# Two 16-head self attentions rebuilt: values as matmul weights in column groups, scores ahead of transposes, softmax by biased exponentials with their own row sums

## The reference, cut to what matters

```python
scores = jnp.einsum('bthd,bshd->bhts', q, k)
scores = scores * jnp.tril(jnp.ones((T, T)))
attn = jax.nn.softmax(scores / T ** 0.5, axis=-1)
out = jnp.einsum('bhts,bshd->bthd', attn, v).reshape(B, T, H * Dh)
return out @ Wo
```

```python
scores = jnp.einsum('bhqd,bhkd->bhqk', q, k) * 32 ** -0.5
attn = jax.nn.softmax(scores, axis=-1)
out = jnp.einsum('bhqk,bhkd->bhqd', attn, v)
return lora_linear(out.transpose(0, 2, 1, 3).reshape(B, L, H * hd), Wo, bo, Bo, Ao)
```

## Time and profile before

| | us |
|---|---|
| median of 3 runs (2780.65 to 2783.71) | 2782.24 |
| profiled execution, device time | 2780.92 |
| its span | 2779.2 |
| first attention: scores from, last exponentials to | 202.8, 308.3 |
| second attention: scores from, last exponentials to | 1587.8, 1698.3 |

### The profile page before, as it was taken

One profiled execution on the slowest core, in us unless ns is written; L12 is line 12 of the kernel. 1 busy time (PEld: TensorE's weight loads), 2 busy tenths in 40 slices (PEclk: granted clock), 3 DMA queues, 4 the chain that ended last, 5 costly groups with the idle time before them and its releaser, 6 DMA issues. The chain is left out here.

```text
span 2779.2 us, 48345 instructions
## 1 busy us (share of the span) xinstructions
PE 2516.6 (91%) x14891; PEld 2020.3 (73%) x14892; DVE 1668.5 (60%) x3141; ACT 1132.1 (41%) x2442; POOL 932.6 (34%) x942
## 2 busy tenths in 40 slices
PE   7999778769899989799997998998999999899998
PEld 7888655558688877578875777774665678788887
DVE  4537746669776656667675566864434325666564
ACT  2113256623343324455453133755555521444443
POOL 4213101124332235422333111753333322355555
PEclk9999889889899979899998898999999989999999
DMA  5444132125522045477774432344222031566664
GB/s 190 154 143 101 27 101 67 45 83 163 175 75 64 14 144 186 131 220 228 198 219 108 112 78 77 115 134 145 74 63 76 20 130 55 153 163 163 162 152 83
DMA packets 289277, 332.88 MB, mean 120 GB/s; under 512 B 147445, under 2 KB 202693, under 8 KB 287312
## 3 DMA queue, kind: packets, MB, share of 16 engines
q1 hardware_dynamic: 217904, 252.57, 28.9%
q0 software_dynamic: 20640, 51.74, 9.3%
q10 hardware_dynamic: 50560, 26.34, 3.3%
HBM read 233.86 MB, written 96.72 MB: 119 GB/s over the span
## 5 line engine op out<-in xcount | busy, mean ns | idle before, releaser
L898 PE MATMUL e_psum<-e_up_hi,hT_hi 128*128 x672 | 245.5, 365 | 21.3 <-DVE hT_lo L867 16.3
L900 PE MATMUL e_psum<-e_up_hi,hT_lo 128*128 x672 | 237.1, 353 | 0.0
L899 PE MATMUL e_psum<-e_up_lo,hT_hi 128*128 x672 | 236.5, 352 | 0.0
L1905 POOL TENSOR_TENSOR joint_a_p<-joint_a_p,joint_a_rinv 112x487 f32<-112x487 f32 x128 | 125.2, 999 | 196.1 <-DVE joint_a_rinv L1951 195.7
L1565 POOL TENSOR_TENSOR self_a_p<-self_a_p,self_a_mx 112x448 f32<-112x448 f32 x96 | 96.0, 1000 | 207.7 <-DVE self_a_mx L1622 207.7
L898 PEld LDWEIGHTS e_psum<-e_up_hi,hT_hi 128*128 128x128 f32 x672 | 127.7, 190 | 44.0 <-issue 32.6
L1956 DVE TENSOR_REDUCE joint_a_mx<-joint_psum 112x1 f32<-112x487 f32 x128 | 85.0, 664 | 122.1 <-PE joint_psum L1926 122.0
L794 ACT ACTIVATE e_gate<-e_psum 128x352 f32<-128x352 f32 (+1 forms) x86 | 44.4, 516 | 256.5 <-PE e_psum L900 256.0
L873 DVE TENSOR_TENSOR hT_lo<-e_psum,hT_hi 128x256 fp32r<-128x256 f32 (+2 forms) x138 | 55.6, 434 | 142.1 <-ACT hT_hi L812 142.1
L1656 ACT ACTIVATE self_a_p<-self_a_p 112x448 f32<-112x448 f32 x128 | 71.6, 575 | 165.7 <-POOL self_a_p L1565 115.4
L900 PEld LDWEIGHTS e_psum<-e_up_hi,hT_lo 128*128 128x128 f32 x672 | 127.6, 190 | 11.5
(11 more groups left out here) (565 smaller groups left out, 7419.9 us busy)
## 6 DMA issues: line engine op xcount, KB each, us to landing
e_up_raw<-in_L_ffn_w SPq DMA_DIRECT2D x64, 512.0 KB, 5.0
e_up_raw<-in_L_ffn_w SPq DMA_DIRECT2D x64, 352.0 KB, 3.7
e_dn_raw<-in_L_ffn_w SPq DMA_DIRECT2D x16, 1024.0 KB, 5.5
q_all<-p_p_t_stage ACTq DMA_DIRECT2D x56, 256.0 KB, 2.3
e_dn_raw<-in_L_ffn_w SPq DMA_DIRECT2D x16, 512.0 KB, 4.0
x_q<-q_all SPq DMA_DIRECT2D x8, 896.0 KB, 5.1
v_ctx<-front_c_v_stage SPq DMA_DIRECT2D x24, 250.0 KB
x_others<-k_ctx SPq DMA_DIRECT2D x8, 750.0 KB, 4.9
```

The costliest lines, as they stand in the source:

```text
L898: pe.matmul(out, lhs[0], rhs[0], start=k == 0, stop=False)
L899: pe.matmul(out, lhs[0], rhs[1], start=False, stop=False)
L900: return pe.matmul(out, lhs[1], rhs[0], start=False, stop=k == n_k - 1)
L1905: pool.tensor_tensor(p[:, r, :], p[:, r, :], rinv[:, r:r + 1].to_broadcast([T, S]), ALU.mult).then_inc(p_ready, 1)
```

## The change

Both attentions use a new class, `HeadSelfAttentionPart`; `QkvPart`, `OutNormPart` and the order function are the same. It differs so:

- **Order.** In A of step s PE has the scores of s first and the transposes of s-2 behind.
- **Softmax.** DVE takes the maxima and multiplies them by -scale (`neg`, 112x4). ACT takes one exponential per head, 112x112, with `neg` as bias and the row sum as its accumulator: eight per step instead of two. With a mask it reads the masked copy in SBUF, without one it reads the scores' banks in PSUM, so there the next scores wait for `exp_done` (before: for DVE's subtraction).
- **Row sums.** In B of the next step DVE inverts eight sums at once, and POOL multiplies both items by them, in both attentions. The transposes wait for POOL (`p_ready`).
- **Values.** V becomes the weights (112x32 per head), the transposed probabilities stream, and the heads of four items go to four 32-row groups of one PSUM bank. It is done once per sequence, in B of odd steps, and gives the result already transposed: `OutNormPart` then skips L2268 (`turned`), and the ones' column goes.

```diff
+class HeadSelfAttentionPart:
+        def gpsimd(pool):
...
+                yield
+                for i in pair(step, 1):
+                    pool.wait_ge(rinv_ready, i // W + 1)
+                    pool.tensor_tensor(p[:, i % RING, :, :], p[:, i % RING, :, :], rinv[:, i % RING, :].unsqueeze(2).to_broadcast([T, group, T]),
+                                       ALU.mult).then_inc(p_ready, 1)
...
+        def tensor(pe):
...
+                both = pair(step)
+                if both:
...
+                    reuse(pe, mask_done if mask else exp_done, both[-1] - N_S + 1)
+                    for j in range(group):
+                        for i in both:
+                            last = pe.matmul(ps[0:T, s_banks[i % N_S], j * T:(j + 1) * T], q[rows_of(i), b % 2, j, :],
+                                             k[rows_of(i), b % 2, j, :], start=True, stop=True)
...
+                for i in pair(step, LT):
+                    pe.wait_ge(p_ready, i + 1)
+                    reuse(pe, pt_ready, i - N_T + 1)
+                    for j in range(group):
+                        last = pe.transpose(ps[0:T, t_banks[i % N_T], j * T:(j + 1) * T], p[:, i % RING, j, :], core.ident[0:T, 0:T])
...
+                yield
+                at = step - LT
+                if at >= 0 and at % n_steps == n_steps - 1:
...
+                    pe.wait_ge(pt_ready, (b + 1) * n_items)
+                    for j in range(group):
+                        for i in range(b * n_items, (b + 1) * n_items):
+                            h = j * group + i % n_items
+                            last = pe.matmul(ps[rows_of(i), o_banks[b % N_O], j * T:(j + 1) * T], v[:, b % 2, h * dh:(h + 1) * dh],
+                                             pt[:, i % PT, j, :], start=True, stop=True)
+                    last.then_inc(pv_done, 1)
...
+        def vector(dve):
...
+                    dve.tensor_reduce(mx[:, i % RING, :], src, AX.X, ALU.max).then_inc(mx_ready, 1)
+                    dve.wait_ge(mx_ready, i + 1)
+                    dve.tensor_scalar(neg[:, i % RING, :], mx[:, i % RING, :], -scale, None, ALU.mult).then_inc(neg_ready, 1)
+                yield
+                before = pair(step, 1)
+                if before:
+                    at = before[0] % RING
+                    dve.wait_ge(exp_done, before[-1] + 1)
+                    dve.reciprocal(rinv[:, at:at + W, :], rsum[:, at:at + W, :]).then_inc(rinv_ready, 1)
...
+        def scalar(act):
...
+                yield
+                for i in pair(step):
+                    act.wait_ge(neg_ready, i + 1)
...
+                    for j in range(group):
+                        src = p[:, i % RING, j, :] if mask else ps[0:T, s_banks[i % N_S], j * T:(j + 1) * T]
+                        last = act.activation(p[:, i % RING, j, :], src, ACT.Exp, bias=neg[:, i % RING, j:j + 1], scale=scale,
+                                              accum_out=rsum[:, i % RING, j:j + 1])
+                    last.then_inc(exp_done, 1)
...
-                    a = SelfAttentionPart(g, "a", *head_qkv(p), float(T) ** -0.5, (2, 3), (4, 5), (6, 7), "tril", ALU.mult)
+                    a = HeadSelfAttentionPart(g, "a", *head_qkv(p), float(T) ** -0.5, (2, 3), (4, 5), (6, 7), "tril")
...
-                a = SelfAttentionPart(g, "a", *head_qkv(p), 32.0 ** -0.5, (2, 3), (4, 5), (6, 7))
+                a = HeadSelfAttentionPart(g, "a", *head_qkv(p), 32.0 ** -0.5, (2, 3), (4, 5), (6, 7))
```

101 lines of the change are left out of this document (100 added, 1 removed).

## The result

The changed kernel takes 2823.42 us (median of 3 runs, 2822.01 to 2829.43) against 2782.24 before: a ratio of 1.0159 (95% interval 1.0134 to 1.0183), 41 us slower. The forecast was 2797, with a range of 2777 to 2817. The direction was right; the size was not, and it lies outside the range.

What follows compares the result with a forecast made beforehand. PE was taken to bound the second attention's steps 6 to 15, DVE the first's. Span 2779.2 + 5.5 (second) + 3.7 (first) + 7 (clock) = 2795.4, given as 2797 us in measured time; range 2777 to 2817.

Steps and rivals of the forecast that it cites:

- The clock: Both attentions' loops: 38 us of PE work at full clock, about a fifth as much again at 1.2 GHz: +7, range 0 to 30.
- vanish, since PE waits: Second attention, steps 6 to 15: PE's saving of 3.4 us per sequence brings nothing, because PE waits.
- Behind step 15: Stretch from step 15's scores to the last transposes: +0.8 us in the first attention, +1.0 in the second.
- POOL's leg: POOL multiplies two items by the inverted sums before the transposes: 1.83 us; the first attention's last step pays it again, +0.8.
- Second attention, steps 6 to 15: Loop from scores through exponentials to next scores: 5.2 us even, 5.7 odd, 8.6 turn steps; 62.3 us against 53.6, +8.7.
- The wait for the banks: Second attention: next scores need both PSUM banks, which ACT's exponentials of the step before still read; closes the 5.2 us loop.
- First attention, steps 6 to 15: Cycle of two steps 14.2 instead of 12.73 us, DVE waiting 2.1 us at each turn step: +5.1.
- Exponentials: ACT, one per head at 112 columns with accumulator: 0.33 us each, eight in 2.66 a step; range 0.2 to 0.56.
- start: Before step 6, PE's shorter values save time: -2.2 us in the first attention, -4.2 in the second.
- The scores' place: Scores ahead of the transposes on PE: said to cost PE nothing.
- The sums: Span 2779.2 + 5.5 + 3.7 + 7 = 2795.4; with 1.7 above span and 1.3 to the median, given as 2797 us.
- The rival that named the half clock for most of the stretch: PE stays at 1.2 GHz (+19), or exponentials cost 0.45 us and more (+9, second attention): 2810 to 2820, chance 0.16.

Runs made afterwards that it cites:

- h6_filled_less: Changed kernel plus idle PE transposes where PE waits, also behind step 15, with 8 instead of 22 before the second attention's odd-step scores: 2796.83 us (1.0050).
- e5_early_sums: Changed kernel, but DVE inverts the previous step's sums at the end of its piece A instead of in piece B: 2809.98 us (1.0095).
- h3_filled_tail: Changed kernel plus idle PE transposes in steps 6 to 15 (22 before the second attention's odd-step scores) and behind step 15: 2801.46 us (1.0066).
- h2_filled: Changed kernel with early sums, DVE's subtraction, values and V's load a step later, plus 8 idle transposes before every step's scores from 6: 2794.38 us (1.0039).
- e4_subtracted: Changed kernel, but in the second attention DVE subtracts the maxima into SBUF, so the next scores wait for DVE, not the exponentials: 2807.78 us (1.0089).
- h5_second_unfilled: First attention as before the change; second rebuilt with early sums and DVE's subtraction, no idle transposes: 2780.78 us (0.9993 of the kernel before).

## Why the prediction was wrong

- **The clock: the step that failed.** "I take about a fifth, +7; the range is 0 to 30." Measured: 23, that is 0.6 of the 38 us of PE's work that I had counted in the loops. My own rows gave the pieces: waits of some 3 us, and the earlier trace rows, where one wait of 1.69 us was followed by 4.44 us of matmuls at mostly half clock. With waits of 1.5 to 3.8 us ahead of seven of the nine scores of steps 7 to 15, the second attention ran at 1.2 GHz for 0.6 of the stretch, not for a fifth. And the overall range, up to 2817, did not reach the end of the clock's own range, because I gave that end little chance.
- **PE as bound again.** The forecast took PE out of the reckoning ("vanish, since PE waits"). Mostly at half clock PE needs 7.4 and 7.6 us in the even steps without a turn and sets their length; at full clock (h6_filled_less) such a step took 5.4, for a loop of 5.2.
- **Behind step 15**: forecast +0.8 and +1.0, measured +9.1 and +8.5; with PE's waits filled still +7.2 and +4.1. This is the second term that was mis-sized. I counted POOL's leg, and gave the wait ahead of it nothing: the reciprocal of step 15's sums stands behind `hT_lo` of step 16 on DVE (7.5 us in the second attention), with no more scores for PE to do in between. e5_early_sums wins back 4.7 and 7.1 us. Of the first attention's +7.2, 2.5 come from where the stretches are cut: the scores of step 15 followed the last turn's transposes by 3.00 us before (values and transposes stood between) and follow them by 0.48 now.
- **Second attention, steps 6 to 15**: the loop was right in kind and nearly in size: 5.4, 5.8 and 8.5 us measured at a held clock for 5.2, 5.7 and 8.6; 64.3 for 62.3. The wait for the banks was there as computed: in the changed kernel the accumulator reading of step 9's last exponential ends at 1674.83, and the scores of step 10 start at 1674.97.
- **First attention, steps 6 to 15**: the cycle was right, 13.9 us in h3_filled_tail against 14.2, and so was DVE's wait in it: 2.2, 2.1 and 2.1 us at the three turn steps of h6_filled_less for the 2.1 computed. Two of them:

```profile
270.00 0.62 DVE L2336 TENSOR_TENSOR hT_lo<-self_psum,hT_hi 128x448 fp32r<-128x448 f32 x1 [2.18 <-ACT hT_hi L2301]
283.85 0.62 DVE L2336 TENSOR_TENSOR hT_lo<-self_psum,hT_hi 128x448 fp32r<-128x448 f32 x1 [2.11 <-ACT hT_hi L2301]
```

But I set the cycle against one cycle before, the 12.73 of the earlier trace rows; by the starts of L2250 the next two took 14.3 and 13.2. At held clock the stretch gains nothing and loses nothing (cut at the last turn's transposes instead of the scores of step 15, it loses 2.7). The +5.9 that the changed kernel shows there is nearly all clock (5.7 by the filled run), so that it is close to the +5.1 is luck.
- **Exponentials** 0.33, forecast 0.33; **start** of the two attentions -1.5 and -4.4 for -2.2 and -4.2: right.
- **The scores' place** was said to cost nothing. True for PE's work; it also hides POOL's leg, 26 us.
- **The sums.** 2795.4 + 1.7 + 1.3 is 2798.4, not 2797. And in the clock paragraph PE's work before is 10.9 of 11 us by the trace (1665.05 to 1676.08), not 10.4; the 7.6 that it leads to stands.

Together: the clock is 16 us over its term, the stretches behind step 15 at held clock 9.5 over, the second attention's steps 6 to 15 2 over, the first's 5 under. That is 23 of the 26 us by which the time was missed; the rest lies outside of the six stretches, in the wrong sum and in what executions differ by.

The rival that named the half clock for most of the stretch (2810 to 2820, chance 0.16) was the true one, and its +19 for the clock is near the 23 measured. It stopped short by what the stretches behind step 15 took. Its other half, dearer exponentials, did not come.

## What to carry to other kernels

Before you take work off TensorE, ask what it will do in the time: if a wait appears in every round (here 1.5 to 3.8 us), price its remaining work in the loop at 1.2 GHz as well, and see whether it is then the bound again. A granted clock of 0.7 in a window whose PE is not saturated was the sign here; a few idle matmuls in the wait are the test, and sometimes the mend. They gave 26.6 us back on the changed kernel (h6_filled_less), and nothing in h2_filled, where they stood in every step. And an instruction that opens a chain (here one reciprocal of 0.19 us for the sums of eight heads) belongs ahead of every wait in its engine's order that does not concern it.

## What the runs showed of the hardware

- With 73 matmul records more, idle transposes, a stretch took 53.5 instead of 61.8 us. Filling all of a wait was not needed: with 8 instead of 22 ahead of the scores of odd steps the clock was 0.89 instead of 0.97 (h6_filled_less, h3_filled_tail), and the stretch 2.4 us shorter.
- Shortening waits was not enough: with no wait over 2.0 us left the clock stayed at 0.72 (e4_subtracted), with waits of up to 4.6 us at 0.74 (h5_second_unfilled).
- Biased exponentials of 112x112 with their sums follow each other at 0.33 us where they read PSUM (second attention), and at 0.37 us where they read SBUF (first attention of the changed kernel):

```profile
281.37 0.38 ACT L1818 ACTIVATE self_a_p<-self_a_p,self_a_neg 112x112 f32<-112x112 f32 x1
...
281.74 0.38 ACT L1818 ACTIVATE self_a_p<-self_a_p,self_a_neg 112x112 f32<-112x112 f32 x1
```

The Trainium skill (TensorE: Matmul & The Clock Gate, Part 1) calls the half clock the default state, which activity lifts. By that rule the filled runs should be granted more clock than the unfilled ones, and they are: 0.87 to 1.00 against 0.68 to 0.78 in steps 6 to 15 of a rebuilt attention.
